# First attention of a fused block: the weighted sums of four heads for both key tiles in one burst every fourth step

## The chip, the cores and the metric

One core of a Trainium2 chip (trn2) runs the whole program. The metric is the time of one execution on the device in microseconds (us), lower is better; the times shown are of several executions of the same compiled kernel.

## The reference

`x` is 4 x 512 x 512 (batches, rows, features), float32. Four layers follow each other, each as x + layer(layernorm(x)): a first attention with a mask that is learned from pairs of rows, a feed-forward layer, a second attention, and the same feed-forward layer again. The change lies in the first attention, behind its mask:

```python
# first attention: B = 4, S = 512, 32 heads of 2 features, K = 64
qkv = jnp.einsum('bsd,ed->bse', xn, Wqkv) + bqkv
q, k, v = heads(split(qkv))                       # (B, 32, S, 2)
scores = jnp.einsum('bhid,bhjd->bhij', q, k) / math.sqrt(2)
scores = scores + mask[:, None, :, :]             # 0 for 51 keys of each row, else -inf
attn = jax.nn.softmax(scores, axis=-1)
ao = jnp.einsum('bhij,bhjd->bhid', attn, v)       # weighted sums
out = jnp.einsum('bsk,dk->bsd', ao.transpose(0, 2, 1, 3).reshape(B, S, K), Wout) + bout
return x + out
```

## The kernel before

The program has five stages, one after the other: pairs of rows (the mask), the first attention, feed-forward, the second attention, feed-forward. In each stage a list of steps is written out in Python, and for each step five small programs (one for each of PE, DVE, ACT, POOL and SP) put down what their engine has to do in it. The order of the list is thus the order on every engine; between the engines only semaphores hold. `order_of_attention_a` (L239) makes the list of the first attention, `attention_a` (L866) the programs.

The work is cut into 8 chunks: chunk c is 16 heads of batch c // 2. For each head (h) the kernel does the following.

- "own_keys" (POOL, L1169): the stacked keys with all heads but this one set to zero, into a ring of 28 buffers (first_keys, more_keys).
- "scores", for each of two pairs of row tiles (PE L998, DVE L1085): two matmuls give 128 rows x 512 keys each into PSUM banks 0 and 1 (pair 0) or 2 and 3 (pair 1); one DVE reduction of both banks gives the rows' maxima. The matmuls wait for the reduction of the same pair of the head before (`maxes_made`). At head 0 of a chunk the mask is put into the banks first (L996); later heads add the difference to the head before.
- "place" (PE L1006, ACT L1121, SP L1185): once for each chunk, when its maxima are there: they are turned, negated, and sent by DMA into the stack of queries, so that the second set of score matmuls has the maximum taken off. The chunk's "exp" steps wait for it.
- "exp", for each half of the keys (`keys` = 0, 1), head, and key tile j = 0, 1 of the half (PE L1017, ACT L1129): one matmul gives the turned scores, 128 keys x 512 rows, in bank 4 (j = 0) or 5 (j = 1); ACT takes the exponential into one of 16 buffers `ex`. The matmul waits until ACT is done with the exponential before in the same bank (`pe.wait_ge(ex_made, i - 1)`), ACT waits for the matmul, and, 16 exponentials later, for the "weighted" step that reads the buffer. At head 0 of a chunk's half, L1015 puts in the mask.
- "weighted", for each group of four heads, key half and key tile j (PE L1049): four matmuls, each with 12 columns of values and ones for weights, in the four column groups of the array (output partitions 0, 32, 64, 96 of bank 6). They are float32 and run as two passes, so that a burst is 8 weight loads and 8 matmuls in the trace. They wait for the last exponential of the group in that tile, and gather a whole chunk in bank 6; ACT then copies it (`ao_t`, L1142).
- After both chunks of a batch: four times "divide" (PE L1059 turns, DVE L1096 and L1098), "feature" (PE L1066, ACT L1146) and "project_a" (PE L1073, DVE L1103 adds to x, then L166 and L167 take the statistics of the row). "turn" (PE L985, ACT L1114) turns the mask of the next batch, "values" (POOL L1157) lays out its values. "early_root" (ACT L183), once in chunk 6, is a square root whose function table has to be loaded, and after it that of the exponential.

The list begins with 36 "scores" pairs (LEAD), by which the maxima run ahead. Then come 7 chunks of 32 steps; step i is `keys, h = divmod(i, 16)`. An even step has one "scores" pair, then its two "exp"; an odd step its two "exp", then a pair. So on PE the order over two steps is: pair, exp, exp, exp, exp, pair, and the next pair follows at once. "place" comes behind the "exp" of a step. When h is 3 modulo 4, the group's two "weighted" steps (j = 0, 1) are put in a queue. In every even step one of them is taken out, behind the "exp": j = 0 when h is 0 modulo 4, j = 1 two steps later. In the odd steps one "side" step (a turn, divide, feature or project) is taken out, between two pairs. When the last "weighted" of a batch is taken out, the steps that finish the batch go to the head of the side queue. The eighth chunk has steps of its own ("last_exp", L1034 and L1135; both tiles j in one ACT instruction over two banks; L1030 is its mask), and among them the start of the feed-forward layer.

Of the kernel before, what the change touches and what calls it, by code (L numbers as in the profile page):

```python
# [73 lines left out]
def build(nc, d):  # L74
    with ExitStack() as ctx:
# [38 lines left out]
        for queue in queues:  # L114
# [6 lines left out]
            queue.wait_ge(p.v_made, B)  # L121
        heads_mem = ctx.enter_context(ExitStack())
        order = order_of_attention_a()
        k.nth = numbered(order)
        heads_stage = attention_a(k, p, a, heads_mem, k.nth)
# [113 lines left out]
def order_of_attention_a():  # L239

    order = [("own_keys", n) for n in range(KEYS_AHEAD)] + [("values", 0)] + [("turn", 0, t) for t in range(NT)]
    side, weighted, places = [], [], []
    maxima = iter([(c, h, pair) for c in range(CHUNKS) for h in range(CHUNK) for pair in range(2)])

    def next_maxima():
        for c, h, pair in [at for at in (next(maxima, None),) if at]:
            order.append(("scores", c, h, pair))
            if pair == 0 and CHUNK * c + h + KEYS_AHEAD < CHUNKS * CHUNK:  # L250
                order.append(("own_keys", CHUNK * c + h + KEYS_AHEAD))
            if (h, pair) == (CHUNK - 1, 1):
                places.append(("place", c))

    def place():

        while places and ("scores", places[0][1], CHUNK - 1, 1) not in order[-3:]:
            order.append(places.pop(0))

    for i in range(LEAD):  # L260
        next_maxima()
        place()
    for c in range(CHUNKS - 1):
        b = c // 2
        if c % 2 == 0 and b + 1 < B:
            side += [("turn", b + 1, t) for t in range(NT)]
        for i in range(2 * CHUNK):
            keys, h = divmod(i, CHUNK)
            if h % 2 == 0:
                next_maxima()  # L270
            order += [("exp", c, keys, h, 0), ("exp", c, keys, h, 1)]
            place()
            if h % 2:
                next_maxima()
            if weighted and h % 2 == 0:
                order.append(weighted.pop(0))
                if order[-1][1:] == (c - 1, 1, CHUNK // 4 - 1, 1) and c % 2 == 0:
                    side[:0] = finish_steps(b - 1)
            if h % 4 == 3:
                weighted += [("weighted", c, keys, h // 4, j) for j in range(2)]  # L280
            if side and i % 2:
                order.append(side.pop(0))
            if (c % 2, i) == (0, 16) and b + 1 < B:
                order.append(("values", b + 1))
            if (c, i) == (CHUNKS - 2, 4):
                order.append(("early_root",))
    beside = iter(FIRST_ROWS)
    for h in range(CHUNK):
        for keys in range(2):
            order.append(("last_exp", h, keys))  # L290
            if weighted:
                order.append(weighted.pop(0))
        order += next(beside, [])
        if h % 4 == 3:
            weighted += [("weighted", CHUNKS - 1, keys, h // 4, j) for keys in range(2) for j in range(2)]
    assert next(beside, None) is None
    order += [("operand", 0, 1), ("operand", 0, 2)] + weighted + side + [("product", 0, 11)]
    for among, steps in FIRST_UNIT:
        order += [(kind, B - 1, t) for kind, t in among] + steps
    return order + first_tail()  # L300
# [6 lines left out]
def finish_steps(b):  # L307
    steps = []
    for t in range(NT + 2):
        if t < NT:  # L310
            steps.append(("divide", b, t))
        if 1 <= t <= NT:
            steps.append(("feature", b, t - 1))
        if t >= 2:
            steps.append(("project_a", b, t - 2))
    return steps
# [945 lines left out]
def first_tail():  # L1262
    return [("difference", 0, 3), ("operand", 0, 7)] + behind(0)
# [1078 lines left out]
```

## Time and profile before

| what | us |
|---|---|
| median of 3 executions | 3141.8 |
| the others of the three | 3140.8, 9992.69 |
| the profiled execution, its own time | 3138.7 |
| its span, first to last instruction | 3137.5 |
| loop over chunks 0 to 6 in it | from 1117 to 1497 |
| rest of the first attention | to 1544 |

The third execution, 9992.69 us, stands far from the rest, and the median isn't touched by it. In the profile, PE is TensorE with its matmuls and PEld its weight loads, DVE is VectorE, ACT is ScalarE, POOL is GpSimd and SP issues DMAs. Times in the timeline count from the first instruction. A piece of the timeline is a run of equal instructions on one engine: its start, how long until the last one ended, how many, and in brackets the idle time ahead of it with what ended it. The end of one matmul lies behind the start of the next, since they are pipelined; the distance of two starts is what a matmul costs. PEclk is the granted TensorE clock as a share of full speed.

### The profile page before, as it was taken

The numbers are of one execution on the slowest core, as the hardware profiler recorded it, in microseconds if no ns is written. First come the engines' busy times: TensorE is split into PE (matmuls) and PEld (weight loads), VectorE is DVE, ScalarE is ACT, GpSimd is POOL, SyncE is SP. The second block draws the span as 40 slices with busy tenths as digits, with TensorE's granted clock in tenths as the row PEclk, the third lists the DMA queues.
The fourth block names the chain that finished last, engine by engine and source line by source line (L and its number), as shares of the span: only waits on it lengthen the run. The fifth ranks groups of instructions, "written<-read, shape, count | busy, mean of one in ns | idle before, by whom it ended". The sixth has DMA issues, their size and how long they took to land. (4 is left out here: it accounts for less than half of the span.)

```text
span 3137.5 us, 56845 instructions
## 1 busy us (share of the span) xinstructions
PE 2981.5 (95%) x22569; PEld 1795.1 (57%) x22569; DVE 2335.7 (74%) x4298; ACT 1771.8 (56%) x2897; POOL 1061.6 (34%) x881
## 2 busy tenths in 40 slices
PE   6999999999999799999899999989999987999999
PEld 3545445444556545444478778844444425887787
DVE  6998999999999877777366676655766766667665
ACT  4988888888889356666643333314443443334332
POOL 1000000000000454533255565504544554565653
PEclk9999999999999789999999999999999988999999
DMA  2000000000000000000112111143332311112111
GB/s 76 2 2 12 2 2 12 2 2 12 2 2 2 1 2 1 2 1 1 35 44 58 51 44 51 44 126 96 81 88 77 93 34 54 44 56 72 53 50 49
DMA packets 105805, 112.93 MB, mean 36 GB/s; under 512 B 8963, under 2 KB 74500, under 8 KB 105157
## 3 DMA queue, kind: packets, MB, share of 16 engines
q1 hardware_dynamic: 102918, 108.61, 12.3%
q8 instruction: 180, 2.95, 0.4%
q10 hardware_dynamic: 2624, 0.69, 0.1%
q14 instruction: 83, 0.68, 0.1%
HBM read 84.76 MB, written 20.97 MB: 34 GB/s over the span
## 5 line engine op out<-in xcount | busy, mean ns | idle before, releaser
L734 DVE TENSOR_SCALAR pair_in<-key_words,row_words 128x512 f32<-128x512 f32 x1792 | 725.8, 480 | 33.6 <-PE ps L620 29.6
L819 ACT ACTIVATE pair_mid<-ps,row_bias 128x512 f32<-128x512 f32 x896 | 589.3, 691 | 114.9 <-PE ps L620 97.4
L620 PE MATMUL ps<-pair_in,w_hi 128*32 128x512 f16 x7168 | 625.7, 390 | 11.7 <-DVE pair_in L734 11.3
L620 PE MATMUL ps<-pair_in,w_lo 128*32 128x512 f16 x3584 | 393.3, 390 | 0.0
L1085 DVE TENSOR_REDUCE maxes<-ps 128x2 f32<-128x1024 f32 x256 | 303.4, 1221 | 96.9 <-PE ps L998 95.8
L620 PEld LDWEIGHTS ps<-pair_in,w_hi 128*32 128x32 f16 x7168 | 256.1, 95 | 205.1 <-issue 37.5
L847 POOL TENSOR_SCALAR_AFFINE_SELECT sim<-sim 128x512 f32<-128x512 f32 x16 | 10.2, 641 | 1030.2 <-ACT sim L836 1030.2
L1129 ACT ACTIVATE ex<-ps 128x512 f32<-128x512 f32 x448 | 243.3, 595 | 119.0 <-PE ps L1017 118.4
L1495 PE MATMUL ps<-ffn_b_hi,ffn_a_hi 128*128 128x512 f32 x904 | 286.1, 398 | 25.1 <-DVE ffn_up L1583 9.1
L1495 PE MATMUL ps<-ffn_b_lo,ffn_a_hi 128*128 128x512 f32 x904 | 282.2, 394 | 1.7 <-DVE ffn_b_lo L1565 1.7
L1495 PE MATMUL ps<-ffn_b_hi,ffn_a_lo 128*128 128x512 f32 x904 | 281.2, 393 | 0.7 <-POOL ffn_a_lo L1726 0.7
L1633 DVE TENSOR_TENSOR x<-x,ps 128x512 f32<-128x512 f32 x256 | 175.6, 686 | 136.2 <-PE ps L1512 133.3
L635 PE MATMUL ps<-pair_mid,w_slide 128*32 128x512 f32 x2048 | 247.3, 592 | 0.0
L2240 ACT ACTIVATE ex_b<-ps 128x512 f32<-128x512 f32 x256 | 147.4, 598 | 168.4 <-PE ps L2084 162.3
L2172 DVE TENSOR_REDUCE maxes_b<-ps 128x1 f32<-128x512 f32 x256 | 169.3, 682 | 85.8 <-PE ps L2069 85.3
L1495 PEld LDWEIGHTS ps<-ffn_b_hi,ffn_a_hi 128*128 128x128 f32 x904 | 169.1, 190 | 69.6 <-DVE ffn_up L1583 11.7
L1726 POOL TENSOR_TENSOR ffn_a_lo<-ffn_sums,ffn_a_hi 128x1024 fp32r<-128x1024 f32 x60 | 148.4, 2473 | 171.0 <-ACT ffn_a_hi L1648 171.0
L1693 ACT ACTIVATE ffn_gate<-ffn_gate 128x512 f32<-128x512 f32 x60 | 37.9, 632 | 277.0 <-DVE ffn_gate L1590 277.0
L1495 PEld LDWEIGHTS ps<-ffn_b_lo,ffn_a_hi 128*128 128x128 f32 x904 | 171.4, 190 | 39.8 <-DVE ffn_b_lo L1565 3.6
L1495 PEld LDWEIGHTS ps<-ffn_b_hi,ffn_a_lo 128*128 128x128 f32 x904 | 171.4, 190 | 37.5 <-POOL ffn_a_lo L1726 1.1
L2022 POOL TENSOR_TENSOR ex_sum<-ex_sum,ex_b 128x512 f32<-128x512 f32 x124 | 156.9, 1283 | 81.9 <-ACT ex_b L2240 81.7
L620 PEld LDWEIGHTS ps<-pair_in,w_lo 128*32 128x32 f16 x3584 | 128.6, 95 | 88.2 <-issue 27.6
(240 smaller groups left out, 5434.0 us busy)
## 6 DMA issues: line engine op xcount, KB each, us to landing
ffn_raw_up<-in_w_ffn SPq DMA_DIRECT2D x64, 512.0 KB, 4.0
ffn_raw_down<-in_w_ffn SPq DMA_DIRECT2D x64, 256.0 KB, 2.7
q_stack<-halves SPq DMA_DIRECT2D x48, 256.0 KB, 5.1
k_stack<-halves SPq DMA_DIRECT2D x48, 256.0 KB, 5.9
halves<-hi_b SPq DMA_DIRECT2D x16, 512.0 KB, 2.6
halves<-lo_b SPq DMA_DIRECT2D x16, 512.0 KB, 3.6
out<-x SPq DMA_DIRECT2D x4, 1024.0 KB, 4.4
x<-in_x SPq DMA_DIRECT2D x6, 512.0 KB, 6.1
```

What stands on the lines that cost most here:

```text
L620: s = nc.tensor.matmul(ps[32 * quarter:32 * quarter + 32, bank + which, :], w_part[:, at_w:at_w + 32], words.rearrange("p (s two) -> p s t ...
L635: s = nc.tensor.matmul(ps[32 * c:32 * c + 32, 6 + w, :], p.w3_slide[:, 30 - 2 * r:62 - 2 * r], p.pair_mid[:, n % NG, half, :], start=r == ...
L734: s = nc.vector.tensor_scalar(p.pair_in[:, (4 * n + i) % N_PAIR, :], p.key_words[:, b % 2, :], p.row_words[:, b % 2, row:row + 1], None, A ...
L819: nc.scalar.activation(p.pair_mid[:, n % NG, which, :], ps[:, bank + which, :], ACT.Relu, bias=bias).then_inc(p.mid_made, 1)
L1085: nc.vector.tensor_reduce(maxes[:, c % 2, 2 * pair:2 * pair + 2, h], ps[:, 2 * pair:2 * pair + 2, :], AX.X, ALU.max).then_inc(maxes_made, 1)
L1129: nc.scalar.activation(ex[:, i % N_EX, :], ps[:, EXP_BANKS[j], :], ACT.Exp, scale=2.0 ** -0.5).then_inc(ex_made, 1)
L1495: i = nc.tensor.matmul(bank, a_part[:, s % 2, a_at, h, :], b_part[:, place(operand), h, :], start=opens and (which, m, h) == (0, 0, 0), st ...
L1633: nc.vector.tensor_tensor(x[:, n, :], x[:, n, :], ps[:, 6 + t % 2, :], ALU.add).then_inc(x_added, 1)
L1726: nc.gpsimd.tensor_tensor(lo, source, hi.bitcast(F32), ALU.subtract).then_inc(w_lo_made, 1)
L2022: engine.tensor_tensor(ex_sum[:, g, :], first, ex[:, i % N_EX, :], ALU.add).then_inc(done, 1)
L2172: nc.vector.tensor_reduce(maxes[:, n % 2, g, t:t + 1], ps[:, O1_BANKS[i % 3], :], AX.X, ALU.max).then_inc(max_made, 1)
L2240: nc.scalar.activation(ex[:, i % N_EX, :], ps[:, O2_BANKS[i % 2], :], ACT.Exp, scale=SCALE).then_inc(ex_made, 1)
```

## The change

In an even step whose h is 0 modulo 4 both "weighted" steps that wait in the queue are taken out, j = 0 and then j = 1; when h is 2 modulo 4, none is. The test for the end of a batch looks at the last one taken, as before. Nothing else is changed: neither the buffers nor the waits of a step, nor the eighth chunk.

```diff
@@ -272,8 +272,9 @@
             place()
             if h % 2:
                 next_maxima()
-            if weighted and h % 2 == 0:
-                order.append(weighted.pop(0))
+            if weighted and h % 4 == 0:
+                order += weighted[:2]
+                del weighted[:2]
                 if order[-1][1:] == (c - 1, 1, CHUNK // 4 - 1, 1) and c % 2 == 0:
                     side[:0] = finish_steps(b - 1)
             if h % 4 == 3:
```

## Rows read from the trace of the kernel before

**Rows 1.** The page, first part: each engine's busy time.
```profile
PE 2981.5 (95%) x22569; PEld 1795.1 (57%) x22569; DVE 2335.7 (74%) x4298; ACT 1771.8 (56%) x2897; POOL 1061.6 (34%) x881
```

**Rows 2.** Busy time by stretch: PE, PEld, DVE, ACT, POOL; clock, DMA share, GB/s.
```profile
1117.00:1497.00 380.00, 376.45 (x1955) 184.93 (x1955) 284.99 (x298) 259.89 (x488) 158.73 (x108) 1.00 0.01 1
1450.00:1460.00 10.00, 9.69 (x45) 4.65 (x45) 6.42 (x12) 6.31 (x13) 0.00 (x0) 0.83 0.01 2
1500.00:1510.00 10.00, 7.98 (x40) 3.58 (x32) 0.69 (x1) 9.53 (x12) 0.00 (x0) 1.00 0.37 108
```

**Rows 3.** Waits, 1117 to 1497: waiter <- releaser: us, times, longest.
```profile
ACT ex L1129 <- PE ps L1017: 118.4, 210, 1.5
PEld ps L1017 <- ACT ex L1129: 110.3, 165, 2.0
...
PE ps L1017 <- ACT ex L1129: 2.2, 3, 1.6
```

**Rows 4.** Groups of instructions, 1117 to 1497: count, busy us, mean ns, idle before.
```profile
L1129 ACT ACTIVATE ex<-ps 128x512 f32<-128x512 f32 x448 | 243.3, 595 | 119.0 <-PE ps L1017 118.4
...
L1103 DVE TENSOR_TENSOR x<-x,ps 128x512 f32<-128x512 f32 x12 | 8.1, 677 | 0.0
...
L1049 PEld LDWEIGHTS ps<-ex,v_aug 128*12 128x12 f32 x880 | 13.6, 90 | 32.6 <-issue 32.6
```

**Rows 5.** Timeline of a plain pair of steps: start, us, engine, what, count, idle.
```profile
1181.79 1.05 PE L1049 MATMUL ps<-ex,v_aug 128*12 128x512 f32 x8
1182.77 0.73 PE L1017 MATMUL ps<-qs,more_keys 112*128 112x512 f32 x2
1183.33 1.08 PE L998 MATMUL ps<-first_keys,qs 112*128 112x512 f32 x4
...
1183.99 2.36 DVE L1085 TENSOR_REDUCE maxes<-ps 128x2 f32<-128x1024 f32 x2 [0.72 <-PE ps L998]
...
1184.25 0.68 PE L1017 MATMUL ps<-qs,more_keys 112*128 112x512 f32 x2
...
1184.86 1.05 PE L1049 MATMUL ps<-ex,v_aug 128*12 128x512 f32 x8
```

**Rows 6.** Timeline of PE at the end of chunk 7, where bursts follow bursts.
```profile
1541.18 0.60 PE L1049 MATMUL ps<-ex,v_aug 128*12 128x512 f32 x2
...
1542.04 0.60 PE L1049 MATMUL ps<-ex,v_aug 128*12 128x512 f32 x2
```

**Rows 7.** Timeline at the start of chunk 0: no burst yet, then the first.
```profile
1119.89 0.63 PE L1017 MATMUL ps<-qs,first_keys 112*128 112x512 f32 x2
1120.32 2.27 ACT L1129 ACTIVATE ex<-ps 128x512 f32<-128x512 f32 x4 [0.15 <-PE ps L1017]
...
1120.97 0.98 PE L1017 MATMUL ps<-qs,first_keys 112*128 112x512 f32 x2 [0.45 <-ACT ex L1129]
...
1121.79 0.63 PE L998 MATMUL ps<-more_keys,qs 112*128 112x512 f32 x2
...
1123.01 0.63 PE L1017 MATMUL ps<-qs,first_keys 112*128 112x512 f32 x2
1123.45 1.09 ACT L1129 ACTIVATE ex<-ps 128x512 f32<-128x512 f32 x2 [0.15 <-PE ps L1017]
...
1126.34 0.62 PE L1017 MATMUL ps<-qs,first_keys 112*128 112x512 f32 x2
```

**Rows 8.** Timeline of PE: behind a feature, early root, next burst, last chunk's start.
```profile
1257.80 0.70 PE L998 MATMUL ps<-first_keys,qs 112*128 112x512 f32 x2 [0.21 <-DVE maxes L1085]
...
1450.31 0.98 PE L1017 MATMUL ps<-qs,more_keys 112*128 112x512 f32 x2 [1.56 <-ACT ex L1129]
1451.22 1.44 PE L1049 MATMUL ps<-ex,v_aug 128*12 128x512 f32 x8
...
1455.93 0.62 PE L1049 MATMUL ps<-ex,v_aug 128*12 128x512 f32 x4
...
1496.77 0.60 PE L1030 MATMUL ps<-mask_t,ident_bf 128*128 128x512 bf16 x2 [0.20 <-DMA qs<-max_t]
```

## The prediction

> **What bounds the kernel now.** I read the page's first part: PE is busy for 95% of the span, DVE for 74%, ACT for 56% [rows 1]. The share is only an average, so I went to the stretch that the change touches. The first attention's steady part, from the first exponential to the end of its seventh chunk, lasts 380 us, and PE is marked busy for 376.45 us of it, at full clock; DVE has work for 285 us, ACT for 260 us [rows 2]. The reader is to see that a microsecond more or less on PE here is a microsecond of the kernel. Next come the waits of the stretch. The long ones are those of ACT and DVE for PE; the one in the other direction that is worth a look is that of PE's weight loads for ACT's exponentials, 110.3 us in 165 times, the second longest row, while the matmuls themselves waited for them 3 times, 2.2 us in all [rows 3]. So nearly all of it is hidden behind the matmul that still streams; what it says is how close PE runs behind ACT: the next score matmul often stands at the door before its bank is read.
>
> The last view is the timeline. I write E for the two matmuls of a step's "exp" (banks 4 and 5, one each for ACT), M for one pair of a "scores" step (two matmuls, two banks, one DVE reduction), B for a burst of one "weighted" step. A plain pair of steps runs B E MM E on PE and repeats after 3.07 us, from 1181.79 to 1184.86 [rows 5]. Its terms: MM follow each other in 0.92 us for four matmuls (1183.33 to 1184.25), 0.23 us each, so eight matmuls are 1.84 us. A burst that directly follows another takes 0.86 us, twice 0.43 (1541.18 to 1542.04) [rows 6]. 3.07 - 1.84 - 0.86 leaves 0.37 us. Of this some 0.04 is the second matmul of the second E, which comes late for ACT (that row has 0.68 us where one without this wait has 0.63 [rows 7]); the other 0.33 us is the way into and out of the four narrow column groups: the load of L1049 can't be drawn ahead of the matmul before it, nor that of L1017 ahead of the burst (0.98 us from burst to matmul, not 0.86).
>
> **The change, part by part.** No instruction comes or goes. In the loop over chunks 0 to 6 there are 110 bursts (880 weight loads of L1049, eight to a burst [rows 4]). They now stand as 55 double bursts, at every fourth step. Four steps were B E MM E B E MM E and become BB E MM E E MM E.
>
> Saved: one way in and out, 0.33 us, for each double burst: 55 x 0.33 = 18.2 us.
>
> Added: where the second burst stood, two E now follow each other with nothing between. The third E needs the banks of the second, and ACT has only just been given them. The trace of before has this very order at the start, where no burst is ready yet [rows 7]: E starts at 1119.89, ACT starts 0.43 us later (1120.32), needs 0.60 us for the first of the two (mean 595 ns [rows 4]), and the next E starts at 1120.97, 1.08 us after the one before, "idle 0.45 <-ACT". Its second matmul is late again, and M begins at 1121.79. Four matmuls took 1.90 us where 4 x 0.23 = 0.92 are work: a stall of 0.98 us. With the burst between (same rows, one turn of the next mask in each) the two steps last 3.33 us (1123.01 to 1126.34), without it 3.12 us (1119.89 to 1123.01). So taking the burst out gives 0.21 us, and setting it behind the other costs 0.86 us. Net +0.65 us for a double burst whose steps have other work among the M.
>
> In plain steps two of the 0.04 us waits vanish into this: 16 x 0.23 + 2 x 0.86 + 0.33 + 0.98 = 6.71 us, against 2 x 3.07 = 6.14 us. Net +0.57 us.
>
> Of the 55, some 23 stand in steps with side work (chunk 0 one, chunks 2 and 4 eight each, chunk 6 six), 32 in plain ones: 23 x 0.65 + 32 x 0.57 = 33.2 us.
>
> Bounds of the stall: PE can't be held longer than ACT needs for the two exponentials of the second E, 0.43 + 0.49 + 0.60 = 1.52 us after its start for both (ACT's second follows the first after 0.49, as 1.09 us for two less 0.60) [rows 7], where 0.46 is E's own work, so at most 1.06. From below, ACT might be given the second E earlier than there; even so the first bank costs 1.08 - 0.46 = 0.62 us. Net per double burst thus +0.25 to +0.73 us, 14 to 40 us in all. I take 0.98, measured in the same order of instructions.
>
> What else moves. DVE: its two reductions per MM take 2.36 us and start 0.66 us behind the first matmul (1183.33, 1183.99) [rows 5], so both are done 3.02 us behind it. By the terms above MM now start 2.82 us and 3.89 us apart instead of 3.07 twice (0.92 us for MM and 1.90 us for the stalled E E, and the rest of 6.71), and the second M of the next group needs its banks another 0.46 us later, at 3.28 us: it fits with 0.26 us to spare in plain steps. Beside a projection, whose add of 677 ns [rows 4] and the statistics behind it (about as long again, my estimate) stand between the two reductions, it doesn't quite; a wait of 0.21 us for DVE exists there already [rows 8], and the twelve such places may grow by 0.1 us each, +1 us. ACT's buffers: an exponential of the group after next waits for the burst of this one; the first tile's burst comes at the same step as before and the second's two steps earlier, so nothing there gets later. The copy of the weighted sums and the steps that finish a batch start two steps earlier; they are cut into the same odd steps, nobody waits for them before the next batch, cost nothing. SP's only transfer in the loop follows "place", which keeps its place in the order. At the very end it matters: the last double burst is ahead of the last "place", the burst that it loses is behind it, where PE waits for the transfer anyway (0.20 us, L1030 [rows 8]); there the price is 0.86, not 0.65, +0.2 us. On the other side, in chunk 6 the early square root holds ACT with two table loads, and PE waits 1.56 us for it at 1450.31 [rows 8]; a double burst stands right ahead and covers up to 0.86 us of that, and the low clock behind it (0.83 over 10 us [rows 2]) may go: -1.5 us. Together about nothing: +33 us.
>
> The Trainium skill, page "TensorEngine Tiling (Array Packing)", section "PSUM Bottleneck", warns that tiling makes TensorE faster but not the reading of PSUM, and advises both ScalarE and VectorE for it. By that rule it is the pace of the two readers that would decide, as in the rows of 1119.89; the trace agrees, with 0.98 us.
>
> The sum: the profiled execution's own time is 3138.7 us (span 3137.5), with the change 3138.7 + 33 = 3171.7 us. The median shown, 3141.8, lies 3.1 us above it, so a median of 3174.8 us, say 3175, 1.05% slower. A measurement of this kernel tells about 2% from no change, so this is within it.
>
> **Rivals.** (a) Only the ways in and out count, and the kernel gets faster. The mechanism is the 0.33 us at L1049; it decides if the stall between the E stays under 0.33 us, which needs ACT to be done with the first bank within 0.46 + 0.33 = 0.79 us of E's start. For it: PE had no visible idle time in 376 of 380 us. Against: 1.08 us measured. 3141.8 - 18.2 = 3123.6, say 3124 us. The same page, section "Key Properties", has it that a change of tiling mode drains TensorE; by that alone the change would win just these switches. The rows show the switch, at 0.33 us, and show the stall that outweighs it. Chance 0.05.
>
> (b) Nothing changes, because the stall eats waits that stood elsewhere (behind side work, for DVE) and the two sides cancel: 3142 us. Against: PE's waits in the loop sum to a few us [rows 2]. 0.04.
>
> (c) DVE takes over: with the M closer together the second pair of each MM waits for its reduction, some 0.5 us more for each double burst (3.02 us and a semaphore's way, with 0.7 us of other work between, against 3.28): 55 x 0.5 = 27 us more, 3202 us. For it: DVE is busy for 285 of 380 us, and 4 x 1.18 = 4.7 us of 6.7 are its. Against: the 0.26 us to spare, and at 1121.79 M did not wait for it. 0.05.
>
> (d) The stall lets the granted clock fall. For it: behind the 1.56 us of idle time at 1450.31 it was 0.83 over 10 us, between the levels 2.4 and 1.2 GHz, and a burst took 1.44 us for 1.05 [rows 2, 8]. Against: at 1500 to 1510 PE was busy for only 7.98 of 10 us, its ACT at 9.53, and the clock was 1.00 [rows 2]. The price at 1451.22: to the next burst (1455.93) 4.71 us, where two steps with work among them took 3.33 and some more: about 1.2 us; 55 times, 66 us: 3175 + 66 = 3241 us. 0.04.
>
> **How the numbers follow.** My forecast, 3175 us, has 0.82, with its own bounds 14 and 41 us: 3156 to 3182, a little wider above since DVE's waits can only add. The 80% range is 3152 to 3190 us: it leaves out (a), (b), (d) and (c) at its full size. Faster by over 2%: 0.01 (even (a) is 0.6%). Slower by over 2%, above 3204.6: (d), and (c) if it is a bit dearer, 0.06. Within 2%: 0.93.
>
> **What the new profile would show.** Right: L1049 x16 in one piece, 1.92 us long; per four plain steps 6.7 us; each second E with a wait for ACT L1129 of 0.4 to 0.5 us ahead of it; the row "PE ps L1017 <- ACT ex L1129" grown from 2.2 us to 20 or 30 us with some 55 or 110 waits; PE's busy share of the loop down to 93% or so; clock 1.00; the loop 413 us long instead of 380 and all behind it later by 33 us, otherwise unchanged. A wait of L998 for DVE in plain steps would speak for (c), a clock under 1.00 in them for (d). The forecast is wrong if the loop isn't longer by 14 us at least.

## The result, and the profile after

| | before | after |
|---|---|---|
| median, us | 3141.07 (5 runs: 3136.24 to 3141.8, and 9992.69) | 3174.34 (5 runs, 3169.71 to 3178.42) |
| profiled execution, own time / span | 3138.7 / 3137.5 | 3175.34 / 3174.1 |

The ratio is 1.0111, 95% interval 1.0100 to 1.0123: 33.3 us slower by the medians. 3175 us was forecast. Single executions that stand far above all others of their kernel (9992.69 us here, 4874.32 us in experiment 5) are left out of the ratios. (Lines of the order's function move down by one in the changed kernel: L1017 is L1018, L1049 is L1050, L1129 is L1130.)

The timeline of four plain steps of the changed kernel, as [rows 5]:

```profile
1181.85 1.91 PE L1050 MATMUL ps<-ex,v_aug 128*12 128x512 f32 x16
1183.68 0.73 PE L1018 MATMUL ps<-qs,more_keys 112*128 112x512 f32 x2
1184.25 1.08 PE L999 MATMUL ps<-first_keys,qs 112*128 112x512 f32 x4
...
1184.91 2.36 DVE L1086 TENSOR_REDUCE maxes<-ps 128x2 f32<-128x1024 f32 x2 [1.52 <-PE ps L999]
...
1185.17 0.68 PE L1018 MATMUL ps<-qs,more_keys 112*128 112x512 f32 x2
...
1185.61 2.28 ACT L1130 ACTIVATE ex<-ps 128x512 f32<-128x512 f32 x4 [0.30 <-PE ps L1018]
...
1186.26 0.99 PE L1018 MATMUL ps<-qs,more_keys 112*128 112x512 f32 x2 [0.41 <-ACT ex L1130]
1187.09 1.08 PE L999 MATMUL ps<-first_keys,qs 112*128 112x512 f32 x4
...
1187.75 2.35 DVE L1086 TENSOR_REDUCE maxes<-ps 128x2 f32<-128x1024 f32 x2 [0.48 <-PE ps L999]
...
1188.01 0.62 PE L1018 MATMUL ps<-qs,more_keys 112*128 112x512 f32 x2
1188.57 1.91 PE L1050 MATMUL ps<-ex,v_aug 128*12 128x512 f32 x16
```

Read it from burst to burst: 1181.85 to 1188.57 is 6.72 us (6.71 forecast, 6.14 before). Sixteen matmuls of L1050 stand in one piece; the matmul behind them starts 1.83 us after the first of them, not 2 x 0.98, so 0.13 us of the switch (the way into and out of the column groups) can be seen saved here. Then the open gap, as I call the place where two E follow each other with nothing between: from 1185.17, the second E, to 1187.09, the next M, four matmuls take 1.92 us, with ACT's four exponentials in one unbroken piece. The reductions come two by two, 2.84 us apart and then 3.87 us.

The waits of the stretch, as [rows 3], and its busy times, as [rows 2]:

```profile
ACT ex L1130 <- PE ps L1018: 136.1, 153, 1.6
...
PEld ps L1018 <- ACT ex L1130: 100.5, 182, 1.3
...
PE ps L1018 <- ACT ex L1130: 24.4, 58, 0.8
...
PE ps L999 <- DVE maxes L1086: 2.0, 4, 0.9
```
```profile
1117.00:1530.00 413.00, 385.65 (x1943) 189.98 (x1959) 287.89 (x302) 261.60 (x489) 158.69 (x108) 1.00 0.01 1
```

The row of PE's own matmuls waiting for ACT went from 2.2 us in 3 times to 24.4 us in 58, about one for each of the 55 double bursts. The weight loads' row, so large before, even fell: what it had shown were loads that came late but in the cover of a matmul. PE is busy for 93.4% of the loop, at a clock of 1.00. DVE's row is as good as empty.

Where the time went, by the starts of the first matmul of each chunk (L1015 or L1016) in both timelines:

| stretch, us | before | after |
|---|---|---|
| chunk 0 | 51.82 | 56.02 |
| chunks 1, 3, 5 (plain) | 51.55, 51.54, 51.57 | 56.13, 55.58, 55.66 |
| chunks 2, 4 (side steps) | 57.73, 57.76 | 63.38, 63.34 |
| chunk 6 (side steps, early root) | 58.26 | 61.46 |
| loop in all | 380.2 | 411.6 |
| chunk 7, to the first feed-forward product | 47.1 | 48.8 |

Of the 36.6 us between the two spans the loop has 31.3, the start of chunk 0 1.5, chunk 7 1.7 and all behind it 2.0. The medians differ by 33.3 us; executions of one kernel differ from each other by several us, so a forecast that is met within 1 us has luck in it.

### The profile page after: what moved, and what is told of

Read it like the earlier page. It is cut to its first block and busy times, and to the rows that moved or that the text cites. A ratio compares the mean times of both kernels' runs of the same rounds, so it can differ in the third digit from the quotient of the medians.

```text
span 3174.1 us, 56827 instructions
## 1 busy us (share of the span) xinstructions
PE 2994.4 (94%) x22551; PEld 1797.9 (57%) x22569; DVE 2336.8 (74%) x4298; ACT 1773.2 (56%) x2897; POOL 1061.5 (33%) x881
## 5 line engine op out<-in xcount | busy, mean ns | idle before, releaser
L1130 ACT ACTIVATE ex<-ps 128x512 f32<-128x512 f32 x448 | 243.4, 595 | 142.4 <-PE ps L1018 136.1
```

What stands on the lines that cost most here:

```text
L1130: nc.scalar.activation(ex[:, i % N_EX, :], ps[:, EXP_BANKS[j], :], ACT.Exp, scale=2.0 ** -0.5).then_inc(ex_made, 1)
```

## The experiments

The yardstick is the length of a plain (odd) chunk, eight double bursts, beside the whole time. The ratio of each run is to the kernel before on the same chip, whose median was 3140 to 3141 us each time.

**1. Four bursts at a time.** Against the changed kernel:

```diff
-            if weighted and h % 4 == 0:
-                order += weighted[:2]
-                del weighted[:2]
+            if weighted and h % 8 == 0:
+                order += weighted[:4]
+                del weighted[:4]
```

> Four bursts in one at every eighth step (h = 0 modulo 8), else as the changed kernel. Theory: against the kernel before each eight steps save three ways in and out (3 x 0.33) and leave three gaps open (3 x 0.98): +1.8 to +1.95 us, 27 times, about 3192 us (3185 to 3200); three waits for ACT of 0.4 us in eight steps. Rival (the number of switches decides and the double burst is bad for a reason of its own): with half the switches of the changed kernel no more than 3174 us, by the switches alone 3165 us.

3195.05 us (ratio 1.0178, 1.0158 to 1.0198), an odd chunk 58.4 to 58.5 us. PE's timeline shows the gaps one after the other:

```profile
1182.73 0.99 PE L1018 MATMUL ps<-qs,more_keys 112*128 112x512 f32 x2 [0.45 <-ACT ex L1130]
...
1185.56 0.99 PE L1018 MATMUL ps<-qs,more_keys 112*128 112x512 f32 x2 [0.45 <-ACT ex L1130]
...
1187.87 3.62 PE L1050 MATMUL ps<-ex,v_aug 128*12 128x512 f32 x32
```

Half the switches, half again as many open gaps: the gaps decide. The loop over chunks 0 to 6 takes 429.5 us for 411.6: 18.0 us for 27 more open gaps and 27 switches less, 0.67 us each, for 0.98 - 0.33 = 0.65 expected.

**2. The double burst moved by one E.** It stands ahead of the exp of its step, so that both E-E gaps are open; number and length of the bursts stay.

```diff
+            if weighted and h % 4 == 0:
+                order += weighted[:2]
+                del weighted[:2]
...
             order += [("exp", c, keys, h, 0), ("exp", c, keys, h, 1)]
             place()
             if h % 2:
                 next_maxima()
-            if weighted and h % 4 == 0:
-                order += weighted[:2]
-                del weighted[:2]
```

> The double burst moved by two matmuls: ahead of the exp of its step, between a scores pair and the exp, and no longer between two E. As many bursts and switches as in the changed kernel. Theory: now both gaps between E and E are open in four steps, a second stall of 0.98 us: 7.7 us for four plain steps, 3174 + 55 x 0.98 = about 3228 us (3218 to 3236). Rival (only length and number of the bursts count): 3174 us.

3228.38 us (1.0284, 1.0264 to 1.0305), an odd chunk 63.1 to 63.2 us: 54 us more for 55 open gaps by the medians, 0.98 us each; in the profiled executions the loop is 51.3 us longer, 0.93 us each. The second gap has come up right behind the burst:

```profile
1187.55 1.91 PE L1050 MATMUL ps<-ex,v_aug 128*12 128x512 f32 x16
1189.38 0.74 PE L1018 MATMUL ps<-qs,more_keys 112*128 112x512 f32 x2
1190.57 0.99 PE L1018 MATMUL ps<-qs,more_keys 112*128 112x512 f32 x2 [0.45 <-ACT ex L1130]
```

**3. Half the bursts left out.** In chunks 0 to 6 the bursts of j = 1 are not issued; the text on record says what else is missing.

```diff
+            if c < CHUNKS - 1 and j == 1:
+                return
...
-            s.then_inc(weighted_done, 1)
+            s.then_inc(weighted_done, 1 if c == CHUNKS - 1 else 2)
```

> In chunks 0 to 6 the burst of the second key tile (j = 1) is left out of each double burst, so that half of the weighted sums is missing; the first one gives both its signals (and 0.001 is added to the copied sums, so that no denominator is zero). 55 single bursts are left, at every fourth step. Theory: of each double burst just the second burst's 0.86 us goes, and the stall of 0.98 us stays: 3174 - 47 = about 3127 us (3122 to 3133), 5.85 us for four plain steps. So against the kernel before, with 110 bursts, leaving out 55 of them wins only some 14 us. Rival (PE's time is the sum of its work, and a burst costs 0.86 + 0.33 us wherever it stands): 3141 - 55 x 1.19 = 3076 us.

3129.99 us, 0.9971 of before (0.9960 to 0.9982). Half the work of the bursts is gone, and the kernel is only 10 us faster than with all of it: in the kernel before, the second burst of each group did its work in time that PE otherwise loses.

**4. A pair between the two E.** The obvious cure for the open gap:

```diff
-            if h % 2 == 0:
+            if h % 2 == 0 or h % 4 == 3:
                 next_maxima()
             order += [("exp", c, keys, h, 0), ("exp", c, keys, h, 1)]
             place()
-            if h % 2:
+            if h % 4 == 1:
                 next_maxima()
```

> The changed kernel, but in the burst-free odd step (h = 3 modulo 4) the scores pair comes ahead of the two exp, so that the order is BB E MM E M E M E. Theory (PE stalls where two E stand side by side, since ACT needs 1.08 us from the start of one E until its first bank is free): between E and E there is now always a pair, 0.92 us from start to start, so each of the two short gaps stalls for 0.16 to 0.3 us in place of one stall of 0.98 us; four plain steps take 6.1 to 6.35 us and not 6.71, and the time is about 3146 us (3138 to 3156), the waits 'PE ps L1018 <- ACT ex' nearly gone. Rival (the long double burst itself starves ACT or DVE, whatever the order behind it): 3174 us as in the changed kernel, 6.7 us for four steps. Rival (DVE is the limit): waits of L999 for DVE appear, and the time stays over 3165 us.

> The kernel before with the same edit of the order and single bursts: B E MM E B M E M E. A control for the edit alone. Theory: one gap of each four steps has a pair alone between two E, 0.92 us for the 1.08 that ACT needs, so 0.1 to 0.3 us more than 6.14 us: 3141 + 6 to 16, about 3150 us. If the reordering were good in itself, and not by filling the gap that the double burst leaves open, this kernel would be faster than 3141 us too.

The control came out as expected, 3152.12 us (1.0040, 1.0025 to 1.0055). The cure did not: 3168.63 us (1.0090, 1.0073 to 1.0107), and a plain odd chunk got longer, 56.7 us; four steps take 6.92 us. Only chunks 2 and 4 became shorter (61.3 us). The timeline of four plain steps:

```profile
1188.10 0.73 PE L1018 MATMUL ps<-qs,more_keys 112*128 112x512 f32 x2
...
1188.67 1.09 PE L999 MATMUL ps<-first_keys,qs 112*128 112x512 f32 x4
...
1189.33 4.62 DVE L1086 TENSOR_REDUCE maxes<-ps 128x2 f32<-128x1024 f32 x4 [2.29 <-PE ps L999]
...
1189.60 0.67 PE L1018 MATMUL ps<-qs,more_keys 112*128 112x512 f32 x2
...
1190.61 0.73 PE L999 MATMUL ps<-first_keys,qs 112*128 112x512 f32 x2 [0.34 <-DVE maxes L1086]
...
1191.18 0.62 PE L1018 MATMUL ps<-qs,more_keys 112*128 112x512 f32 x2
...
1191.83 0.70 PE L999 MATMUL ps<-first_keys,qs 112*128 112x512 f32 x2
...
1192.37 0.88 PE L1018 MATMUL ps<-qs,first_keys 112*128 112x512 f32 x2
```

PE no longer waits long for ACT, it waits for DVE: from 1119 to 1490 us the waits of PE's own matmuls for ACT fell from 22.2 us (changed kernel) to 0.8, those for DVE rose from 0.8 to 15.9 us in 47 times. DVE has four reductions in one piece of 4.62 us, and idle time of 2.29 us under each double burst. I had worked with ACT alone.

**5. The pairs spread over all four steps.** One pair ahead of the exp of every step, M E BB M E M E M E:

```diff
-            if h % 2 == 0:
-                next_maxima()
+            next_maxima()
             order += [("exp", c, keys, h, 0), ("exp", c, keys, h, 1)]
             place()
-            if h % 2:
-                next_maxima()
```

> The changed kernel with one scores pair ahead of the two exp in every step: M E BB M E M E M E. In the run with BB E MM E M E M E the four reductions came back to back (4.62 us) from the first MM on, and the third pair waited 0.34 us for DVE; here the pairs are spread over all four steps and the first one follows the double burst. Theory (two readers with two places each: PE may start an E 1.08 us after the last, and an M 1.94 us after the last but one): E follow each other every 1.1 us in the three short gaps, no pair waits for DVE, four plain steps take 6.3 us, an odd chunk 52 to 53 us, the time about 3149 us (3143 to 3156). Rival (a double burst costs what it costs, 6.7 us, in any order): 3168 to 3174 us.

3162.64 us (median of three; 1.0072, 1.0055 to 1.0088), an odd chunk 55.6 us, four plain steps 6.77 us: PE's waits for DVE are as good as gone, and nothing is won in plain steps. The E follow each other after 1.08, 1.29 and 1.18 us, not 1.1:

```profile
1188.20 0.62 PE L1015 MATMUL ps<-qs,more_keys 112*128 112x512 f32 x2
...
1188.63 3.46 ACT L1127 ACTIVATE ex<-ps 128x512 f32<-128x512 f32 x6 [2.07 <-PE ps L1015]
...
1189.28 0.99 PE L1015 MATMUL ps<-qs,more_keys 112*128 112x512 f32 x2
...
1190.57 0.88 PE L1015 MATMUL ps<-qs,more_keys 112*128 112x512 f32 x2
...
1191.75 0.88 PE L1015 MATMUL ps<-qs,first_keys 112*128 112x512 f32 x2
```

The step I left out: an E that is late at all has both its matmuls late. The second follows the first by ACT's 0.49 us, not by PE's 0.23 (the pieces last 0.99 and 0.88 us, not 0.62), and the next M waits behind it. From there PE goes at ACT's pace until the next burst, with six exponentials in one unbroken piece. From [rows 7], the second bank of an E is free 0.43 + 0.49 + 0.60 + 0.05 = 1.57 us after its start; less 0.23 for the first matmul of the next E and 0.46 for its own two, a gap must, by this estimate, hold nearly 0.9 us of other work to cost nothing; MM (0.92) or a burst (0.86 and the switch) does, one M (0.46) doesn't.

**6. A side step in the gap.** The side step of h = 3 modulo 4 stands ahead of that step's exp:

```diff
+            if side and h % 4 == 3:
+                order.append(side.pop(0))
             order += [("exp", c, keys, h, 0), ("exp", c, keys, h, 1)]
...
-            if side and i % 2:
+            if side and h % 4 == 1:
                 order.append(side.pop(0))
```

> The changed kernel with the side step of h = 3 modulo 4 moved from between the two pairs to between the two E that stand side by side; the other side steps stay. Theory (the open gap of 0.98 us takes in other PE work for nothing): each such side step costs nothing any more, 0.28 us for a turn, divide or feature, 0.87 us for a projection; odd chunks stay at 55.6 us, chunks 2 and 4 go from 63.4 to about 60 us, in all 8 to 10 us less, about 3165 us (3161 to 3169). Rival (a gap isn't filled, it moves): 3174 us.

Chunks 2 and 4 went to 61.4 and 61.3 us, 2.0 less each and not 3.4; the odd ones took 56.15 us. The time, 3170.99 us (1.0100, 1.0083 to 1.0117), can't be told from the changed kernel's; in the profiled execution the loop is 4.9 us shorter, for 8 to 10 expected. The gap takes in other work, if less than expected. Where the rest went stands in the trace: the side steps now come closer behind the division (L1101, L1099 in the changed kernel) that they wait for.

```profile
1234.95 0.44 PE L1062 MATMUL ps<-ident,ao_t 128*128 128x128 f32 x2 [0.80 <-DVE ao L1101]
```

There are two such waits of 0.8 us in each of the chunks 2, 4 and 6, and none in the changed kernel: 1.6 us for a chunk, where 1.4 us were missing.

**7. The readers made faster, one by one.** ACT takes the exponential of half the columns; DVE the maxima of half the keys; both; and both in the kernel before. (These kernels don't compute the right result. Left out of the cut below: POOL fills the buffers `ex` once where ACT writes only half of them, and with half the maxima the exponential has another scale.)

```diff
-            nc.vector.tensor_reduce(maxes[:, c % 2, 2 * pair:2 * pair + 2, h], ps[:, 2 * pair:2 * pair + 2, :], AX.X,
+            nc.vector.tensor_reduce(maxes[:, c % 2, 2 * pair:2 * pair + 2, h], ps[:, 2 * pair:2 * pair + 2, 0:S // 2], AX.X,
...
-            nc.scalar.activation(ex[:, i % N_EX, :], ps[:, EXP_BANKS[j], :], ACT.Exp,
+            nc.scalar.activation(ex[:, i % N_EX, 0:S // 2], ps[:, EXP_BANKS[j], 0:S // 2], ACT.Exp,
```

> The changed kernel, but in chunks 0 to 6 ACT takes the exponential of only 256 of the 512 columns, the rest of the buffers stays at the ones that POOL writes once at the start; so half the rows get no softmax there. PE's work and order are the same. Theory (the stall is ACT's duration): with some 0.37 us for 0.60 the first bank is free 0.86 us after E's start, the stall between two E shrinks from 0.98 to about 0.45 us, and an odd chunk takes 51 to 52 us in place of 55.6. Rival (the stall is PE's own, from the order or the semaphore): 55.6 us. The loop is what counts, not the total, since POOL's filling at the start delays the first keys by some 10 to 25 us.

> The changed kernel, but DVE takes the maxima over only 256 of the 512 keys (and the exponentials get a scale of 2 to the -10, so that they stay finite; the same instruction otherwise). DVE's reduction takes about 0.7 us for 1.22. ACT as in the changed kernel. Theory (in the changed kernel ACT alone sets the stall between two E, DVE has some 0.17 us to spare behind it): an odd chunk still takes 55.6 us, the time is 3168 to 3175 us. Rival (DVE is part of the stall): an odd chunk under 54 us.

> The changed kernel with both readers halved: exponentials of 256 of 512 columns, maxima over 256 keys. With the exponentials alone halved an odd chunk still took 55.50 us, since then the fourth matmul pair waited for DVE. Theory (the two readers are bounds one right behind the other): only with both gone does the loop get shorter; the gap between two E costs 0.4 to 0.5 us in place of 0.98, four plain steps take 6.2 to 6.3 us, an odd chunk 51.3 to 52.5 us, the time about 3144 us (3138 to 3150). Rival (a third thing, PE's own order or the semaphores, holds the loop): 55 us for an odd chunk, 3160 us or more.

> The kernel before with both readers halved in the same way. Theory (there PE never waits for a reader by more than 0.04 us at a time, and the burst between two E is what covers them): almost nothing changes, 3135 to 3141 us, an odd chunk 51.0 to 51.5 us. Rival (the readers cost something in the kernel before too): under 3130 us.

| kernel | us | an odd chunk, us |
|---|---|---|
| changed | 3174.34 | 55.6 to 56.1 |
| changed, ACT halved | 3162.11 | 55.5 |
| changed, DVE halved | 3154.45 | 56.0 to 56.1 |
| changed, both halved | 3127.87 | 52.7 |
| before | 3141.07 | 51.5 to 51.6 |
| before, both halved | 3118.04 | 50.7 to 50.9 |

The totals of the last three experiments hold some 15 to 19 us that I had not thought of: with half the reduction the 36 leading pairs are done sooner, and chunk 0 starts at 1099 to 1102 us and not at 1117 or 1118. That is the greater part of why all three came out under their ranges; the chunks are free of it. There the misses are others: with ACT halved I had expected 51 to 52 us and got 55.5; with both halved 52.7 lies just over, and the kernel before with both, 50.8, just under what was expected. In the chunks ACT's relief alone brings next to nothing in plain steps, DVE's alone nothing, both together 3 us; the kernel before, with the same two readers, has only 0.8 us to win. Even so the double burst doesn't pay: with both readers halved the changed kernel needs 1.9 us more for an odd chunk than the kernel before. In the timeline with ACT halved the E-E gap has shrunk from 1.08 to 0.87 us, as expected, and the fourth M waits in its place (1.46 us for 1.08 for the same four matmuls):

```profile
1209.09 4.78 DVE L1089 TENSOR_REDUCE maxes<-ps 128x2 f32<-128x1024 f32 x4 [1.90 <-PE ps L1002]
1209.35 0.63 PE L1021 MATMUL ps<-qs,more_keys 112*128 112x512 f32 x2
...
1210.22 0.78 PE L1021 MATMUL ps<-qs,more_keys 112*128 112x512 f32 x2 [0.24 <-ACT ex L1134]
...
1210.84 1.46 PE L1002 MATMUL ps<-more_keys,qs 112*128 112x512 f32 x4
```

With the gap's 0.4 us saved and 0.4 us lost at M, four steps last 6.66 us (1206.03 to 1212.69) where they lasted 6.72.

No version here that computes the whole result beats the kernel before.

## Why the prediction was right

- **PE is the bound, and a microsecond on it is one of the kernel.** Right: the loop's 31.3 us are in the total, and what lies behind it is as it was but for 2.0 us.
- **The switch, 0.33 us saved.** In keeping with the runs, measured only by differences: the second burst adds 0.85 us (1.83 - 0.98), the sum over four plain steps, in which the switch is a term, came out at 6.72 us for 6.71, and an open gap costs 0.93 us in the loop of experiment 2 and 0.67 us in that of experiment 1, where each comes with a switch less: 0.26 us.
- **The stall, 0.98 us.** Right, and shown rather than argued: one more open gap for each double burst gave 54 us for 55 (experiment 2; 51.3 us of it in the loop), and one more in eight steps, 27 times, gave 18.0 us in the loop (experiment 1; 21 us by the medians), from which the switch saved is already taken. The row that carried it stood in the trace of before, in the first four steps, where two E had once followed each other because no burst was ready.
- **Plain +0.57, with side work +0.65.** Odd chunks rose by 4.0 to 4.6 us for eight, 0.50 to 0.57 each; chunks 2 and 4 by 5.6 us, 0.70 each; chunk 6 by 3.2 us for eight. Somewhat uneven, with the errors against each other: 31.3 us for 33.
- **The early root gains.** Right: PE's wait of 1.56 us became 0.82 us, and the low clock behind it is gone; chunk 6 rose by 3.2 where chunk 2 rose by 5.65 us.
- **The end of the loop, +0.2 us.** Too small. PE now waits 0.82 us for the transfer of the last maxima, and the clock is low behind it and once more ten us later. Chunk 7 lost 1.7 us. The loss goes with the clock: in the control of experiment 4 chunk 7 took 47.1 us with the clock at 1.00 throughout, in experiment 5 49.3 us, with 0.66 over its first five us. But there its first matmul waited for no transfer, so that this wait lowers the clock isn't shown; what does stays open.
- **Rival (c), DVE takes over.** It didn't, but it was nearer than its 0.05 said. I had given DVE 0.26 us to spare at the fourth pair, and that was too much: with ACT halved the pair came 0.43 us earlier and lost 0.37 us again, so that some 0.06 us were to spare. I had left out the way from the reduction's end through the weight load to the matmul. Whatever brings that pair forward by more runs into DVE (experiments 4 and 7). As a forecast of this change it changes nothing, as a picture of the bound it was half of the truth: two readers of two places each, one right behind the other.
- **Rival (d), the clock.** The loop ran at 1.00 in spite of 24 us of waits.

The profile around the end of the loop, as [rows 8]: the wait, then the clock by stretch (third from last column).

```profile
1529.65 0.63 PE L1031 MATMUL ps<-mask_t,ident_bf 128*128 128x512 bf16 x1 [0.82 <-DMA qs<-max_t]
```
```profile
1530.00:1535.00 5.00, 5.00 (x24) 1.34 (x23) 0.88 (x2) 2.14 (x3) 0.00 (x0) 0.74 0.97 279
...
1540.00:1545.00 5.00, 5.00 (x24) 2.45 (x26) 0.69 (x1) 3.87 (x6) 0.00 (x0) 0.72 0.00 0
```

## What to carry to other kernels

When a producer and its reader share only two buffers, work that is put between two fills can be cover and not overhead: before gathering such pieces into one to save a fixed cost, ask what stands in the gap they leave, and price it by reader latency (from the start of a fill to the freed buffer) less what still fills the gap. Look for the new order in the trace of before: at the start or end of a loop, where a queue is still empty, it has often run once. And when a stall has one named releaser, work out the second reader too, since taking the first away may bring nothing.

## What the runs showed of the hardware

- In the open gap PE's loss is larger than the first wait that the trace names: 0.41 to 0.45 us is written at the matmul, 0.98 us is lost, since the load is late as well, and the second matmul follows at the reader's pace (0.49 us) and not at PE's (0.23 us).
- ACT takes 0.60 us for an exponential of 128 x 512 from PSUM, but two follow each other after 0.49 us; of 128 x 256 they take 381 ns. DVE's reduction of 128 x 1024 takes 1.22 us and repeats after 1.13, that of 128 x 512 takes 689 ns.
- A short idle time of PE can be followed by a low clock, and need not be: behind 1.56 us (before, at 1450.31) it was 0.67 over 5 us, behind 0.82 us (after, at 1529.65) 0.74, while behind 1.32 us (the control of experiment 4, at 1461.17) and the 0.82 us of the early root in the changed kernel, and behind 55 waits of 0.4 us, it stayed at 1.00. In experiment 5 it was 0.66 over 1517 to 1522 us, behind waits of 0.45 and 0.20 us. So the length of the last wait alone doesn't tell it.
